# Attention on Trainium2: copying the context accumulators from PSUM to SBUF before they are normalised

## What is computed

```python
def _L0_attn_ref(x, W_DKV, W_UK, W_UV, W_UQ, W_O):
    c_kv = x @ W_DKV
    k = (c_kv @ W_UK).reshape(b, t, h, hd)
    v = (c_kv @ W_UV).reshape(b, t, h, hd)
    q = (x @ W_UQ).reshape(b, t, h, hd)
    scores = jnp.einsum('bqhd,bkhd->bhqk', q, k) * scale
    scores = jnp.where(causal, scores, -jnp.inf)
    probs = jax.nn.softmax(scores, axis=-1)
    ctx = jnp.einsum('bhqk,bkhd->bqhd', probs, v).reshape(b, t, d)
    return ctx @ W_O

x = _layernorm(x + _L0_attn_ref(x, ...))
x = _layernorm(x + _L0_ffn_ref(x, ...))   # router, top 2 of 8 experts, silu
```

## Time and profile before

| what | us |
|---|---|
| runs of before | 8136.52, 8255.36, 8626.46; median 8255.36 |
| the profiled execution | 8151.16 |
| its span on the slowest core (core 5) | 8149.6 |
| spans of the eight cores | 8087.9 to 8149.6 |
| the attention stage on core 5: first L512 to last L512 | 438.0 to 2797.6 |

### The profile page before, as it was taken

One profiled execution on the slowest core, in us unless ns is written; L12 is line 12 of the kernel. 1 busy time (PEld: TensorE's weight loads), 2 busy tenths in 40 slices (PEclk: granted clock), 3 DMA queues, 4 the chain that ended last, 5 costly groups with the idle time before them and its releaser, 6 DMA issues. The chain is left out here.

```text
span 8149.6 us, 73984 instructions; the slowest of 8 cores (8087.9 to 8149.6 us)
## 1 busy us (share of the span) xinstructions
PE 5955.1 (73%) x23880; PEld 2224.7 (27%) x23880; DVE 2411.5 (30%) x3632; ACT 2044.7 (25%) x2577; POOL 1750.8 (21%) x2420
## 2 busy tenths in 40 slices
PE   3776576576577454469898988887588898988895
PEld 1211111111111011124343433332234343433331
DVE  1312412412422344422222222223322222222225
ACT  0265265265265211111111111111111111111111
POOL 1011111111111101123222232312323222232220
PEclk9787687677677676779998989998799898999786
DMA  4000000000000032131212121212221212121212
GB/s 119 1 3 4 4 3 4 4 3 4 5 2 4 28 106 78 55 105 53 83 42 83 42 83 47 78 57 78 93 73 52 83 42 83 42 83 47 78 37 83
DMA packets 131762, 402.36 MB, mean 49 GB/s; under 512 B 19128, under 2 KB 28472, under 8 KB 131392
## 3 DMA queue, kind: packets, MB, share of 16 engines
q1 hardware_dynamic: 113984, 347.28, 13.8%
q0 software_dynamic: 17408, 50.35, 1.8%
HBM read 347.23 MB, written 50.33 MB: 49 GB/s over the span
## 5 line engine op out<-in xcount | busy, mean ns | idle before, releaser
L986 PE MATMUL ph<-x1h,w1b 128*128 128x512 bf16 x8192 | 1864.1, 392 | 614.3 <-DVE w1b L941 614.3
L1009 POOL TENSOR_TENSOR hsb<-hsb,cwb 128x512 bf16<-128x512 bf16 x1024 | 1206.2, 1178 | 2953.8 <-ACT hsb L1001 2952.2
L1034 PE MATMUL py<-hsb,w2b 128*128 128x512 bf16 x8192 | 1792.5, 382 | 0.0
L440 ACT ACTIVATE probT<-ps_s,biasp 128x1024 bf16<-128x1024 f32 x1152 | 1189.5, 1149 | 935.1 <-PE ps_s L430 924.8
L1050 DVE TENSOR_TENSOR acc<-acc,py 128x512 f32<-128x512 f32 x1024 | 704.0, 688 | 2294.2 <-PE py L1034 2294.2
L1001 ACT ACTIVATE hsb<-ph 128x512 bf16<-128x512 f32 x1024 | 611.4, 597 | 2752.2 <-PE ph L986 2723.7
L986 PEld LDWEIGHTS ph<-x1h,w1b 128*128 128x128 bf16 x8192 | 821.2, 101 | 1654.6 <-issue 790.1
L1034 PEld LDWEIGHTS py<-hsb,w2b 128*128 128x128 bf16 x8192 | 806.0, 98 | 981.3 <-issue 63.2
L512 DVE RECIPROCAL recipS<-ps_cA 1x512 f32<-1x512 f32 x64 | 214.5, 3351 | 1299.9 <-PE ps_cB L494 1299.9
L421 PE MATMUL ps_s<-qT,kTg 64*128 64x512 bf16 x1152 | 500.3, 436 | 110.0 <-DVE rbS L540 55.6
L454 POOL TENSOR_SCALAR_AFFINE_SELECT probM<-probT 128x512 bf16<-128x512 bf16 x512 | 294.7, 609 | 1088.2 <-PE ps_cB L494 746.2
(11 more groups left out here) (157 smaller groups left out, 3013.8 us busy)
## 6 DMA issues: line engine op xcount, KB each, us to landing
stgw<-w SPq DMA_DIRECT2D x512, 512.0 KB, 4.3
xstg<-xT SPq DMA_DIRECT2D x32, 512.0 KB, 4.4
xst<-xT SPq DMA_DIRECT2D x64, 256.0 KB, 5.2
x1f<-resid POOLq DMA_DIRECT2D x64, 256.0 KB, 2.4
xst<-x1f SPq DMA_DIRECT2D x64, 256.0 KB, 6.3
outT<-outf POOLq DMA_DIRECT2D x64, 256.0 KB, 2.4
ctxh<-ctxs POOLq DMA_DIRECT2D x128, 64.0 KB, 2.0
ctxr<-ctxh SPq DMA_DIRECT2D x64, 128.0 KB, 2.8
```

The source lines that it names most:

```text
L440: sc.activation(out=probT[:, sl3 * PW:(sl3 + 1) * PW], in_=ps_s[sl2][:], func=AF.Exp, scale=0.125, bias=biasp[:, hp:hp + 1]),
L986: [te.matmul(ps_h[hidx % 2][:], env_w1b_slice(w1b, s, kd, fm, 2), x1h[:, kd * THL + tch * CH: kd * THL + (tch + 1) * CH], start=(kd == 0), ...
L1009: gp.tensor_mul(out=hsb[:, fm * THL + tch * CH: fm * THL + (tch + 1) * CH], in0=hsb[:, fm * THL + tch * CH: fm * THL + (tch + 1) * CH], in ...
L1034: [te.matmul(ps_y[yidx % 2][:], env_w1b_slice(w2b, s, kf, ym, 1), hsb[:, kf * THL + tch * CH: kf * THL + (tch + 1) * CH], start=(kf == 0), ...
```

## The change

A new SBUF tile cxev (cx_ev in the code, 65 partitions by 2048 f32, 8 KB on each partition) takes a copy of both accumulators at the end of a job: two copies on VectorE, in one scheduled operation `ev` that waits for the last two context matmuls. The reciprocals and the two multiplications read that tile instead of PSUM, and the reciprocals wait for `ev`. Job j+2's first context matmul depends on job j's `ev` instead of on its `cB`.

```diff
--- before.py
+++ after.py
@@ -256,6 +256,7 @@
          nc.sbuf_tensor(f"recipS_{g}", [1, 4 * CH], F32) as recipS, \
          nc.sbuf_tensor(f"rbS_{g}", [64, 4 * CH], F32) as rbS, \
          nc.sbuf_tensor(f"biasp_{g}", [128, 2], F32) as biasp, \
+         nc.sbuf_tensor(f"cxev_{g}", [65, 4 * CH], F32) as cx_ev, \
          nc.sbuf_tensor(f"ksq0_{g}", [128, CH], BF16) as ksq0, \
          nc.sbuf_tensor(f"ksq1_{g}", [128, CH], BF16) as ksq1, \
          nc.sbuf_tensor(f"ctxs_{g}", [64, 4 * CH], BF16) as ctxs:
@@ -370,11 +371,11 @@
             sch.run(f"knrm{g}")
 
         _attn_loop(env, g, kTg, vaug, biasp, probT, probM, recipS, rbS,
-                   ctxs, ktoks, vtoks, vones_tok, bias_tok)
+                   ctxs, cx_ev, ktoks, vtoks, vones_tok, bias_tok)
 
 
 def _attn_loop(env, g, kTg, vaug, biasp, probT, probM, recipS, rbS,
-               ctxs, ktoks, vtoks, vones_tok, bias_tok):
+               ctxs, cx_ev, ktoks, vtoks, vones_tok, bias_tok):
     nc = env.nc
     T, NCH, NKT = env.T, env.NCH, env.NKT
     VW = HG * 65
@@ -478,7 +479,7 @@
                             deps.append(exp_toks[ki])
                             rhs_slot = ('t', (sl3, hb))
                         if kt == 0 and j >= 2:
-                            deps.append(job_dve[j - 2][2])
+                            deps.append(job_dve[j - 2][0])
 
                         def mk_pv(kt=kt, j=j, h_loc=h_loc, hb=hb, nkt=nkt,
                                   rhs_slot=rhs_slot):
@@ -504,21 +505,34 @@
                         else:
                             pslot_free[sl3].append(pt_)
             gkt = base + nkt
+            evdeps = [pv_toks[(gkt - 1, 0)], pv_toks[(gkt - 1, 1)]]
+            if j >= 2:
+                evdeps.append(job_dve[j - 2][0])
+            ev = sch.op("vector", lambda ve, j=j: [
+                ve.tensor_copy(out=cx_ev[:, (2 * (j % 2)) * CH:
+                                         (2 * (j % 2) + 1) * CH],
+                               in_=ps_cA[j % 2][:]),
+                ve.tensor_copy(out=cx_ev[:, (2 * (j % 2) + 1) * CH:
+                                         (2 * (j % 2) + 2) * CH],
+                               in_=ps_cB[j % 2][:])][-1],
+                        deps=evdeps, inc=env.s_dv)
             bsl = (gkt - 1) % 2
-            rdeps = [pv_toks[(gkt - 1, 0)], pv_toks[(gkt - 1, 1)]]
+            rdeps = [ev]
             if j >= 2:
                 rdeps.append(job_bc[j - 2])
             rA = sch.op("vector", lambda ve, j=j:
                         ve.reciprocal(
                             out=recipS[0:1, (2 * (j % 2)) * CH:
                                        (2 * (j % 2) + 1) * CH],
-                            in_=ps_cA[j % 2][64:65, :]),
+                            in_=cx_ev[64:65, (2 * (j % 2)) * CH:
+                                      (2 * (j % 2) + 1) * CH]),
                         deps=rdeps, inc=env.s_dv)
             rB = sch.op("vector", lambda ve, j=j:
                         ve.reciprocal(
                             out=recipS[0:1, (2 * (j % 2) + 1) * CH:
                                        (2 * (j % 2) + 2) * CH],
-                            in_=ps_cB[j % 2][64:65, :]),
+                            in_=cx_ev[64:65, (2 * (j % 2) + 1) * CH:
+                                      (2 * (j % 2) + 2) * CH]),
                         deps=[rA], inc=env.s_dv)
             bdeps = [rB, exp_toks[gkt - 1], psum_free[bsl]]
             b1 = sch.op("tensor", lambda te, j=j, bsl=bsl:
@@ -551,7 +565,8 @@
                         ve.tensor_mul(
                             out=ctxs[:, (2 * (j % 2)) * CH:
                                      (2 * (j % 2) + 1) * CH],
-                            in0=ps_cA[j % 2][0:64, :],
+                            in0=cx_ev[0:64, (2 * (j % 2)) * CH:
+                                      (2 * (j % 2) + 1) * CH],
                             in1=rbS[:, (2 * (j % 2)) * CH:
                                     (2 * (j % 2) + 1) * CH]),
                         deps=cdeps, inc=env.s_dv)
@@ -559,7 +574,8 @@
                         ve.tensor_mul(
                             out=ctxs[:, (2 * (j % 2) + 1) * CH:
                                      (2 * (j % 2) + 2) * CH],
-                            in0=ps_cB[j % 2][0:64, :],
+                            in0=cx_ev[0:64, (2 * (j % 2) + 1) * CH:
+                                      (2 * (j % 2) + 2) * CH],
                             in1=rbS[:, (2 * (j % 2) + 1) * CH:
                                     (2 * (j % 2) + 2) * CH]),
                         deps=[cA], inc=env.s_dv)
@@ -579,7 +595,7 @@
                             in_=ctxs[:, (2 * (j % 2) + 1) * CH:
                                      (2 * (j % 2) + 2) * CH]),
                         deps=[cB], inc=env.s_cd[j % 2], inck=16)
-            job_dve[j] = (rA, e1, cB, dB, cA, dA)
+            job_dve[j] = (ev, e1, cB, dB, cA, dA)
         sch.drain(env.s_cd[0])
         sch.drain(env.s_cd[1])
         sch.run(f"attn{g}")
```

## The result

The changed kernel is slower by a ratio of 1.0074 to the kernel before, 95% interval 1.0044 to 1.0103: some 60 us, within 2%. The medians are 8211.02 us over 26 runs before and 8367.4 us over 23 runs after; they lie further apart than that because many runs of either kernel, more of the changed one's, had one die or both at a lower granted clock for a part of the program, and the ratio leaves these out. The profiled execution after has a span of 8205.6 us against 8149.6.

What follows compares the result with a forecast made beforehand. No single bound overall; between attention jobs, VectorE's time from last context matmul to broadcast is the path. 64 jobs x 1.51 us = 97, clock zero: 8151.2 + 97 = 8248 us, range 8195 to 8400.

Steps and rivals of the forecast that it cites:

- Rivals B and C: B: reciprocals from SBUF become fast, 8085 us, chance 0.03; C: copies hidden or paid for by early release, 8151, chance 0.04.
- Rival A: Between jobs, the low clock lasts longer behind the longer TensorE idle: another 157 us, 8405 in all; chance 0.07.
- steps 1 and 2: At each job's end: two copies ahead of the reciprocals, 1.373 us, and the first reciprocal's semaphore wait behind them, 0.16.
- step 3: Both reciprocals at each job's end read SBUF instead of PSUM, giving back 0.01 us each, 0.02 per job.
- The clock term: Behind each job boundary, shifts in when the clock rises: zero in the sum, 10 us allowed to either side.

## Why the prediction was right or wrong

The mechanism held. VectorE's time between the last context matmul and the broadcast is the path, the earlier release frees nothing, the multiplications don't matter, and the later stages change by some 10 us at most: the copies moved behind the reciprocals cost nothing, doubled they cost again as much per pair, and with one row they cost the same. Rivals B and C are out by the row of the reciprocals (3341 ns) and by the kernel that copies one row only. Rival A is out by the doubled copies, whose loop followed the wait to within 2 us.

The step that failed is the base under the sum, the 8151.2 of "8151.2 + 97 = 8248". It made the forecast a time below the median shown, where the runs showed a kernel slower by a ratio of 1.0074. The sum itself was a tenth too large, 97 us for 87.

- Size, steps 1 and 2 of the change: 1.373 for the copies and 0.16 for the wait behind them. The three starts gave 0.61 + 0.78 = 1.39 together, not 1.53. The pair of copies was priced by two durations added, though its nearest row, L739 with 0.0 idle before it, already was an operation that followed without a wait, and durations of such a pair overlap by 0.08 us; the wait was priced by the row behind the copy L540, 0.16, and came out at 0.10. Less 0.02 for the reciprocals, as step 3 had it, that is 1.37 per job and 87 us where the sum had 97.
- The clock term, zero with 10 us either way, was right: 63 boundaries at 1.37 make 86 us from first to last, and the loop grew by 81 to 88.
- The base. The sum was put on the one profiled execution as though it were the kernel's time. Its later stages held up to 235 us at a granted clock of 0.81, which made it some 30 us longer than an execution without; the trace of before had this level in its clock record, and it was not summed behind the attention stage. Without 0.81 the kernel before has spans up to 8122.7 us, and the 81 to 88 us of the loop make 8204 to 8211. The fastest runs on the chip where the changed kernel was run again beside the kernel before are 8118.30 and 8193.20 us, 75 apart, 0.9%.
- The figure itself. 8248 lies under the median of before that was shown, 8255.36, so as a time beside that median it says that nothing changes, or slightly faster, while the text says 1.2% slower. The 8352 that the text gives for a run standing as the median does was the number consistent with it. That the measured median, 8367.4, lies near is luck: the medians hang on how many runs had a lower clock, and that of before moved from 8255.36 over three runs to 8211.02 over 26.
- The change of 1.2% lies above the measured interval of 0.4 to 1.0%, the chances had it within 2%, and there it is.

What stays open is why the ratio, 1.0074 and then 1.0075, is nearer to 60 us than to the 81 to 88 of the loop. For the second ratio the cores of each run answer most of it. Eight of the nine runs of the kernel before that it rests on take 8118.30 to 8125.37 us, all their cores at a mean clock of 0.834 or more; the ninth takes 8218.23 and has one die at 0.824 to 0.827. Without that one the means are 8120.1 us before and 8197.4 over five runs after: 77 us, 0.95%. For the first ratio the cores of the runs of before are not on record. Their fastest, 8132.24, is 14 us above 8118.30, while the fastest of the changed kernel are alike, 8192.06 and 8193.20; 0.81 in the runs of before, as their first profile had it, would fit, but isn't shown.

From 77 to the loop's 81 to 88 some us are left. On cores without 0.81 the second expert pass takes 2127 us on average in the second profile of before (eight cores, 2113 to 2144) and 2119 and 2115 in the two profiles of the changed kernel (four cores each, 2107 to 2125); the other stages behind the loop agree within 3 us. What shortens that pass is not known.

## What to carry to other kernels

Work put on an engine is priced by its place: the same two copies cost 87 us between the last context matmul and the broadcast that waits for what follows them, and nothing 6.8 us later, behind the reciprocals, where the engine idled. Before a buffer is freed earlier, look in the order for a wait on it. Where none was emitted the release alone gave nothing back; it paid together with an edit that put the freed space to use, the single accumulators. And before a sum is put on a profiled execution, see whether the stages that the change doesn't touch ran at their usual clock, and set the sum beside the same base as the time that it will be compared with.

## What was not expected of the hardware

VectorE operations without a wait between them started 0.60 to 0.61 us apart though listed with 0.68 to 0.69; with a wait for the one ahead they started 0.78 to 0.79 apart, so that wait cost 0.18 us. A copy took as long with one partition as with 65, 689 and 687 ns. A granted clock of 0.81 occurred in some executions of either kernel and of their variants, from 43 us in all on a core to over 4500, mostly behind the attention loop and in some within it, nearly alike on two neighbouring cores; a stretch at it had 307 matmuls in 80 us where 360 went at 1.00.
